# Graph layer with residual norms: the edge pass's output projection in three fp32r passes, its y and scatter one loop turn later

## The reference

```python
q, k, v = split(x @ W_qkv.T + b_qkv)                 # 8 heads of 32
att = einsum('mhd,mhd->mh', q[dst], k[src]) / sqrt(32)
a = softmax of att over the edges with the same dst
x1 = layernorm(x + segment_sum(a * v[src], dst) @ W_ff.T + b_ff)
W = (edge_attr @ W_dist + b_dist) * cut(edge_weight)
agg = segment_sum(embed_table[node_type][src] * W, dst)
out = layernorm(x1 + concat([x1, agg]) @ W_comb + b_comb)
```

## Time and profile before

| | |
|---|---|
| median of 3 runs | 1159.6 us (1157.53 to 1163.75) |
| the profiled execution | 1160.47 us, its span 1158.8 us |
| busy in the span | PE 92%, DVE 84%, ACT 71%, POOL 65% |
| last edge pass | from about 780 us to the end, 49 blocks |
| one turn of it | 7.24 us |
| granted clock of TensorE, 805 to 1115 us | 1.00 |
| busy in 805 to 1115 us | PE 309.86, DVE 270.08, ACT 203.44, POOL 196.53 of 310 us |

### The profile page before, as it was taken

One profiled execution on the slowest core, in us unless ns is written; L12 is line 12 of the kernel. 1 busy time (PEld: TensorE's weight loads), 2 busy tenths in 40 slices (PEclk: granted clock), 3 DMA queues, 4 the chain that ended last, 5 costly groups with the idle time before them and its releaser, 6 DMA issues.

```text
span 1158.8 us, 25565 instructions
## 1 busy us (share of the span) xinstructions
PE 1065.2 (92%) x7302; PEld 983.7 (85%) x7302; DVE 978.6 (84%) x2646; ACT 825.3 (71%) x2513; POOL 754.1 (65%) x607
## 2 busy tenths in 40 slices
PE   4869999999999999999878888879999999999993
PEld 3759999999999999999666666668988888888892
DVE  4978888888888888888978899768888888888882
ACT  2957777777777777777768778894666666666663
POOL 4377777777777777775776776513666666666663
PEclk9979999999999999999989899998999999999997
DMA  4856666666666666665535456746566666666641
GB/s 148 281 213 216 225 228 229 231 225 219 219 219 223 224 228 228 221 228 180 194 129 199 146 190 210 249 155 175 166 178 183 186 184 186 189 187 188 189 140 37
DMA packets 121388, 227.26 MB, mean 196 GB/s; under 512 B 33587, under 2 KB 61486, under 8 KB 121184
## 3 DMA queue, kind: packets, MB, share of 16 engines
q1 hardware_dynamic: 104000, 189.54, 48.4%
q0 software_dynamic: 17248, 36.08, 11.5%
HBM read 137.84 MB, written 93.59 MB: 200 GB/s over the span
## 4 chain that ended last, share of the span: by engine, by line
PE 48%; DVE 28%; issue 11%; ACT 7%; POOL 2%; DVEq 1%; DMA 1%; SPq 0%; ACTq 0%; POOLq 0%
DVE num L1576 5%; PE ps L808 5%; PE ps L829 4%; PE ps L823 4%; PE ps L822 4%; PE ps L867 4%; PE ps L868 4%; PE ps L866 4%; PE ps L824 4%; DVE zeT L1587 3%; DVE yn L1394 3%; DVE stat L1366 3%; DVE agg L1600 3%; DVE est L1613 3%; PE ps L864 2%
## 5 line engine op out<-in xcount | busy, mean ns | idle before, releaser
L699 POOL TENSOR_TENSOR zin<-xin,bff_row 128x1024 f32<-128x1024 f32 x98 | 233.6, 2386 | 81.4 <-DVE stat L1366 69.4
L829 PE MATMUL ps<-w_mix,zT 128*128 128x256 f32 x780 | 197.0, 400 | 32.2 <-ACT zT L1065 31.0
L829 PEld LDWEIGHTS ps<-w_mix,zT 128*128 128x128 f32 x780 | 148.2, 199 | 63.4 <-ACT zT L1065 41.3
L1394 DVE SCALAR_TENSOR_TENSOR yn<-ps,r,bc 128x256 f32<-128x256 f32 x391 | 169.1, 473 | 35.8 <-PE ps L829 21.5
L1081 ACT ACTIVATE junk<-yn 128x256 f32<-128x256 f32 x391 | 158.1, 415 | 43.8 <-DVE yn L1394 43.8
L718 POOL TENSOR_TENSOR ev<-abc,v 128x512 f32<-128x512 f32 x49 | 62.1, 1268 | 136.8 <-DVE zeT L1587 136.8
L708 POOL DMA_INDIRECT xd<-in_x_dram,idx x98 | 94.3, 962 | 76.6 <-PE ps L852 45.3
L1366 DVE BATCH_NORM_STATS2 stat<-zin 128x6 f32<-128x256 f32 x391 | 136.2, 409 | 9.4 <-POOL zin L699 9.4
L1094 ACT ACTIVATE on<-yn,r 128x256 f32<-128x256 f32 x293 | 126.7, 501 | 0.0
L702 POOL DMA_INDIRECT ty<-in_node_type_dram,src_i x98 | 101.8, 1039 | 24.6 <-issue 21.7
L730 POOL DMA_INDIRECT out_dram<-oe,idx x98 | 101.3, 1034 | 25.3 <-issue 19.7
(11 more groups left out here) (208 smaller groups left out, 3330.3 us busy)
## 6 DMA issues: line engine op xcount, KB each, us to landing
xin<-in_x_dram SPq DMA_DIRECT2D x97, 512.0 KB, 4.6
out_dram<-on SPq DMA_DIRECT2D x97, 512.0 KB, 2.9
xd_o<-xdT SPq DMA_DIRECT2D x49, 256.0 KB
v_o<-vT SPq DMA_DIRECT2D x49, 256.0 KB, 2.0
v<-v_o SPq DMA_DIRECT2D x49, 256.0 KB
abc<-a_o SPq DMA_DIRECT2D x196, 64.0 KB
xd<-xd_o SPq DMA_DIRECT2D x49, 256.0 KB, 4.1
sbc<-same_o SPq DMA_DIRECT2D x49, 128.0 KB, 3.8
```

The costliest lines, as they stand in the source:

```text
L699: pool.tensor_tensor(z, xx, bb, ALU.add).then_inc(n_z, 1)
L829: last = mm(ps[0:np_, half(g, j), (j % 2) * D:(j % 2 + 1) * D], zT[:, g % 2, k, j * P:j * P + np_], w_mix[:, k, :], start=k == 0, stop=k = ...
L1394: last = dve.scalar_tensor_tensor(out=yn[0:np_, q, j * D:(j + 1) * D], in0=ps[0:np_, half(g, j), (j % 2) * D:(j % 2 + 1) * D], scalar=r1[0 ...
```

## The change

W_ff is kept as a high and a low part (`wff_hi`, `wff_lo`), and num too: ScalarE's `sum_high` rounds it, GpSimd's `sum_low` subtracts, and `ff` does three fp32r passes instead of one fp32 product. `sum_low(i)` stands between `scatter` and `weigh` on GpSimd, `sum_high(i)` behind the attribute scaling on ScalarE. VectorE's `edge_y` and ScalarE's `edge_squares` are for block `i - 3` instead of `i - 2`; `edge_y` stands ahead of `edge_z` in the turn instead of at its end; `edge_rstd2`, `edge_final` and `scatter` move one block later too.

```diff
-    wff = sb("wff", [P, DC, D])
+    wff_hi, wff_lo = (sb(n, [P, DC, D], F32R) for n in ("wff_hi", "wff_lo"))
...
+    num_hi, num_lo = (z_lo[:, 1, c, :].rearrange("p (c n) -> p c n", c=2) for c in range(DC))
...
+        def sum_low(n):
+            pool.wait_ge(e_num, 2 * (n + 1))
+            pool.wait_ge(e_nh, n + 1)
+            after(pool, e_ffp, n)
+            pool.tensor_tensor(flat(num_lo), flat(num[:, n % 2]), flat(num_hi), ALU.subtract).then_inc(e_nl, 1)
...
-            if within(i - 4):
-                scatter(i - 4)
+            if within(i - 5):
+                scatter(i - 5)
+            if within(i):
+                sum_low(i)
             if within(i + 1):
                 weigh(i + 1)
             if within(i - 1):
...
         def ff(n):
             par = n % 2
-            pe.wait_ge(e_num, 2 * (n + 1))
+            pe.wait_ge(e_nh, n + 1)
+            pe.wait_ge(e_nl, n + 1)
             after(pe, e_z, 2 * (n - 1))
             for c in range(2):
+                to = bank(FF[par])[:, c, :]
                 for k in range(DC):
-                    last = mm(bank(FF[par])[:, c, :], wff[:, k, c * P:(c + 1) * P], num[:, par, k, :], start=k == 0, stop=k == DC - 1)
+                    hi, lo = (w[:, k, c * P:(c + 1) * P] for w in (wff_hi, wff_lo))
+                    mm(to, hi, num_hi[:, k, :], start=k == 0, stop=False)
+                    mm(to, hi, num_lo[:, k, :], start=False, stop=False)
+                    last = mm(to, lo, num_hi[:, k, :], start=False, stop=k == DC - 1)
...
+        def sum_high(n):
+            act.wait_ge(e_num, 2 * (n + 1))
+            after(act, e_ffp, n)
+            act.activation(flat(num_hi), flat(num[:, n % 2]), ACT.Copy).then_inc(e_nh, 1)
...
+            if within(i):
+                sum_high(i)
+            if within(i - 4):
+                edge_final(i - 4)
             if within(i - 3):
-                edge_final(i - 3)
+                edge_squares(i - 3)
             if within(i - 1):
                 edge_z_high(i - 1)
...
-            if within(i - 2):
-                edge_squares(i - 2)
...
+            dve.tensor_tensor(wff_lo[:, k, :], ps[:, A + 1, D:2 * D], wff_hi[:, k, :], ALU.subtract).then_inc(s_wlo, 1)
...
-            after(dve, e_ffp, n - 1)
+            after(dve, e_nh, n - 1)
+            after(dve, e_nl, n - 1)
...
+            if within(i - 4):
+                edge_rstd2(i - 4)
             if within(i - 3):
-                edge_rstd2(i - 3)
+                edge_y(i - 3)
             if within(i - 1):
                 edge_z(i - 1)
...
             if within(i - 2):
                 edge_stats(i - 2)
-                edge_y(i - 2)
```

More of the change, by code:

```diff
@@ L364, in build @@
     e_zp = sem("edge_z_transposed")
+    e_nh = sem("attention_sum_high_parts")
+    e_nl = sem("attention_sum_low_parts")
     e_zh = sem("edge_z_high_parts")
@@ L773, in _ @@
         pool.wait_ge(c_same, 16 * NCH)
-        for i in range(-1, B + 4):
+        for i in range(-1, B + 5):
             if i == 4:
@@ L841, in weight_transposes @@
             after(pe, s_wtc, 3 * k)
-            after(pe, s_wlo, 2 * k)
+            after(pe, s_wlo, 3 * k)
             for r in range(4 * DC):
@@ L1015, in _ @@
                 pe.wait_ge(s_wtc, 6)
-                pe.wait_ge(s_wlo, 4)
+                pe.wait_ge(s_wlo, 6)
                 pe.wait_ge(s_brow, 2)
@@ L1102, in weight_copies @@
             act.activation(w_hi[:, k, 2 * D:3 * D], ps[:, A + 1, 0:D], ACT.Copy).then_inc(s_wtc, 1)
-            act.activation(wff[:, k, :], ps[:, A + 1, D:2 * D], ACT.Copy).then_inc(s_wtc, 1)
+            act.activation(wff_hi[:, k, :], ps[:, A + 1, D:2 * D], ACT.Copy).then_inc(s_wtc, 1)
         def parts(n):
@@ L1218, in _ @@
         scaled(0)
-        for i in range(-1, B + 3):
+        for i in range(-1, B + 4):
             if within(i + 1):
@@ L1687, in _ @@
         dve.wait_ge(c_same, 16 * NCH)
-        for i in range(-2, B + 3):
+        for i in range(-2, B + 4):
             if within(i):
```

## The result

The changed kernel takes 1193.2 us in the median of 4 runs (1186.8 to 1195.5), the kernel before 1160.0 in the same comparison (1157.5 to 1163.8): a ratio of 1.028, 95% interval 1.025 to 1.031. The change is slower. The forecast was 1185 with a range from 1166 to 1238, which holds it; the band of the likeliest case, 1178 to 1192, misses it by 1.2. The profiled execution took 1193.8, its span 1191.9, which is 33.1 more than before.

| stretch | before | after | more | foreseen |
|---|---|---|---|---|
| to the first num scan | 782.73 | 784.23 | 1.5 | 0.4 |
| from there to the second block's zeT | 14.17 | 17.98 | 3.8 | 2 |
| 46 turns to the 48th block's zeT | 333.4 | 359.8 | 26.5 | 22.5 |
| from there to the end of the span | 28.5 | 29.8 | 1.3 | 0 |

A forecast was written before the change was run, and what follows sets the result against it. VectorE and TensorE together were taken to set the 7.24 us turn; a held num makes it 7.73: 46 x 0.49 = 22.5, plus 2 and 0.4 is 25 on 1160.5, giving 1185, range 1166 to 1238 (0.80).

The forecast's parts named there:

- the likeliest case: Last edge pass: num held until 3.37 after zeT by GpSimd's low part of z, turn 7.73; 1178 to 1192, chance 0.42.
- ScalarE's high part is in time: ScalarE in the edge turn: squares take 1.15 from 0.08, the copy 0.61, so z's high part is there at 1.9.
- num meets the low part of z: VectorE and GpSimd: num could start at 2.45 but meets GpSimd's subtraction (2.26 to 3.54), held to 3.37; 0.49 a turn slower.
- rival 4: Mixing product on TensorE: y still waits, the turn stays 7.24, 1163 at worst; chance 0.05 together with no change.
- rival 2: GpSimd's low sums get between the two agg scans: turn 8.85, 1237, or partly 1190 to 1237; chance 0.30 wholly or partly.
- the holder keeps it to its end: VectorE beside GpSimd: a held instruction works as if started 0.17 before the holder's end, so num at 3.54-0.17 = 3.37.
- Rival 1: Nothing is held: num at 2.45, turn 6.81, under TensorE's 6.92; 1143, faster; chance 0.15.
- Rival 3: GpSimd gives way to the scans: low part of z stretched by 1.2 to 1.3, turn 7.55, 1177; chance 0.08.
- TensorE's projection: Output projection: eight matmul slots (1.73 us) become twelve of 0.1175 (1.41), 0.32 saved a turn.
- The small parts: Start and end: 0.4 for the wff_lo subtractions, 2 for the first weighings, 0 for the drain (-1.5 to 1).

The follow-up runs named there:

- z_parts_doubled: The changed kernel with two buffers for the z parts, so the high part need not wait for the block's mixing product: 1228.8 us, ratio 1.060.
- weigh_unbound: The kernel before with one wait removed: GpSimd's weighing no longer waits for the z of two blocks before: 1189.7 us, ratio 1.027.
- y_alone: The kernel before with only y, squares, reciprocal, final scaling and scatter moved one block later, in the change's places: 1188.6 us, ratio 1.024.
- num_from_psum: The changed kernel with num's scans reading their second input from an unused PSUM bank (weighted values left out, projection on one bank): 1199.3 us, ratio 1.032.
- three_passes_alone: The changed kernel with y, squares, reciprocal, final scaling and scatter put back, leaving the three-pass projection and its high and low sums: 1173.2 us, ratio 1.011.
- flags_loaded_early: The changed kernel with the scans' flags copied to PSUM by ScalarE, z parts doubled and the flags loaded a block earlier: 1138.8 us, ratio 0.981.

## Why the prediction was right, and where it was not

**Right in the range and in the cause.** A scan held by GpSimd's low part of z, once a turn, turn 7.75 for a forecast 7.73, TensorE with gaps in place of its full queue. The experiments bear it out from three sides: y's move alone makes it (1188.6), an operand in PSUM removes the held scans (0 in five kernels) and, once the flags are loaded early, the loss (1138.8), and a GpSimd operation sent against scans in the kernel before makes a loss of the same size (1189.7).

**The step that failed** is "ScalarE's high part is in time ... so it is there at 1.9" and with it "num meets the low part of z" with its first scan. The high part ends at 961.22, 2.55 after zeT, since it waits for the mixing product, which waits for y. I had this wait written down, as rival 4, but followed it only along TensorE, where I priced it at 1163 at worst; I didn't ask who waits for the mixing product's buffers. The first scan is therefore free, and the one held is the second. That the sum came out is partly luck, of two errors that cancel: the low part ended 0.71 later than I had it (4.25 after zeT instead of 3.54), and behind it only one scan was left to do instead of two (0.65 to msg instead of 1.30), so that msg starts at 4.72 where I had 4.67. z_parts_doubled shows the step as I wrote it: where only the first num scan is held the turn is 7.70, but rival 2 comes with it in most turns.

**Who is first.** The bound "the holder keeps it to its end" held: 0.18 before the end here, 0.17 from the row I took it from the earlier trace rows. The Trainium skill (page SBUF — State Buffer, section Who interferes with whom), cited in the prediction when no run showed a scan beside a GpSimd operation, says that a VectorE instruction with two SBUF inputs contends with a GpSimd instruction that reads SBUF, and that whichever issues first blocks the other. The runs agree for scans: with two SBUF inputs they are held (44 to 46 in weigh_unbound, y_alone and the change), with one of them in PSUM they are not (0 of 196 in each of five kernels), and in num_from_psum both stand side by side: 0 of 98 num scans with a PSUM input, 17 of 98 agg scans without. Whichever was issued first holds the other.

**Rival 2** was a tie in my sum (6.05 beside 6.04). In the steady turns of the changed kernel the low sums come at 965.63, after both agg scans, because the late low part of z moved the scatters back by some 0.9. In the first turns, without a scatter ahead of it, it did happen: agg pairs of 2.36 us at 792.31 and 799.93. Both lie in the start's stretch that took 3.8 more where I had 2, each 0.97 longer than a free pair; three_passes_alone takes the same 17.98 there and y_alone 14.60, so the 3.8 belongs to the three passes. It happened twice more, in the turn of 8.56 and in the one of 9.45 near 1000 us, whose agg pair and low sums are these:

```profile
1003.21 2.72 DVE L1625 TENSOR_TENSOR_SCAN agg<-sbc,agg,msg 128x256 f32<-128x256 f32 x2
1004.08 1.29 POOL L733 TENSOR_TENSOR z_lo<-num,z_lo 128x512 fp32r<-128x512 f32 x1
```

There num's first scan started only at 1000.18, 0.07 behind the low part of z, and was the held one, as the prediction had it for every turn; the trace doesn't show what made it late. The four held agg scans lost some 4.2 us together: the measured time is the forecast with a little of rival 2. The turn that I gave it, 8.85, is about 9.04 in the turns of z_parts_doubled in which both pairs are held.

**Rival 1** (nothing held, turn 6.81, 1143) was priced about right, though its sum takes 1.4 for the start where the forecast takes 2.4: flags_loaded_early has a turn of 6.80 and 1138.8. It needed edits that the change doesn't have.

**Rival 3** (GpSimd gives way, the low part over 2 us) did not come: the low part takes 1.57 and the scan behind it 1.72. But GpSimd does give way to the scan that is ahead of it, by 0.29 here, and in three_passes_alone it alone does.

**TensorE's projection** takes 1.52 from its first matmul to the transposes (961.34 to 962.86) where I had 1.41; no term hangs on it while TensorE waits.

**The small parts.** The 1.5 to the first num (I had 0.4) is less than the profiled executions differ by at that point: it comes at 776.8 to 785.5 us over all the kernels here, and at 785.5 in y_alone, which has no part of W_ff to subtract. So these runs don't show the 0.4. The 1.3 at the end lies outside the -1.5 to 1 that I gave it and comes with y's move: from the 48th zeT to the end y_alone takes 29.8 too, three_passes_alone 28.9 and the kernel before 28.5. What in y's move makes it was not taken apart.

## What to carry to other kernels

Before moving a step on VectorE, mark which of its instructions read two SBUF operands and see beside which GpSimd operations they will stand: a wait that seems to waste GpSimd's time may be all that keeps the two apart, as in weigh_unbound, and taking a wait or one collision away can move the collision to the next place, as in z_parts_doubled and num_from_psum. Here a place in PSUM for the one operand that all four scans share removed their collisions at once, and with its load early enough TensorE's saving counted at last. Follow each new wait to the buffers that it frees late, not only along the queue that it stands in.

## What was not expected of the hardware

- Two scans directly behind each other are no unit: a GpSimd subtraction issued during the first ran before the second (961.35 to 962.92, the second scan 1.72 us). Issued 0.18 us after the second scan's start it was held itself (1.61 us).
- The one-hot comparison, a TENSOR_SCALAR with one tensor as its input, was held too: in z_parts_doubled it took 1.26 us beside a weighing (956.70), against 0.35 in the changed kernel, and in three_passes_alone 0.47. The scans are not the only instructions to look at.
- Taking a wait away made the kernel slower in two of two cases where scans shared their reads with GpSimd (by 2.7% from the kernel before, by 3% from the changed one); the second of these, the doubled z parts, made no difference where they didn't (1174.1 beside 1175.0).
